# Adjacency of a graph kernel: remainders in neighbouring bf16 elements, two of sixteen one-hots on ScalarE

## What is computed

```python
# N_NODES = 3125
S = jax.ops.segment_sum(X[src], dst, num_segments=N_NODES)
Z = (1.0 + eps[l]) * X + S
```

## Time and profile before

| | us |
|---|---|
| median of three runs | 2696.34 |
| the profiled execution, its own time | 2691.28 |
| its span, first to last instruction | 2689.6 |
| building `adj`: first VectorE instruction of the loop to last ScalarE copy | 104.96 to 361.24 |

### The profile page before, as it was taken

The page is one execution under the profiler, slowest core; times in us unless marked ns, Lnnn a source line. Parts: engine busy times, 40 slices in busy tenths (PEclk is TensorE's granted clock), DMA queues, the critical chain, the costliest instruction groups (busy, mean ns, idle before and its releaser), DMA issues. The chain is left out here.

```text
span 2689.6 us, 46751 instructions
## 1 busy us (share of the span) xinstructions
PE 2128.6 (79%) x9373; PEld 1425.9 (53%) x9374; DVE 1692.9 (63%) x5215; ACT 792.3 (29%) x1810; POOL 1359.2 (51%) x1336
## 2 busy tenths in 40 slices
PE   3577768888799999998799889969996566666666
PEld 1233345555788888885455345534553444455444
DVE  7999951112677777773438634853575677777775
ACT  1233311112122222222111311132113366666663
POOL 2200000000577777771678277727782477777771
PEclk9999978888655555557899899989997777777777
DMA  0000010000444444441211011101113222222221
GB/s 10 3 0 0 0 39 0 0 0 3 120 118 119 119 118 118 119 117 52 39 17 17 9 16 17 17 9 17 17 17 111 62 65 64 66 65 64 65 65 36
DMA packets 197087, 128.42 MB, mean 48 GB/s; under 512 B 138144, under 2 KB 179993, under 8 KB 195872
## 3 DMA queue, kind: packets, MB, share of 16 engines
q0 software_dynamic: 40256, 60.21, 10.4%
q1 hardware_dynamic: 151820, 59.71, 9.0%
q10 hardware_dynamic: 4822, 6.56, 0.7%
HBM read 106.83 MB, written 13.34 MB: 45 GB/s over the span
## 5 line engine op out<-in xcount | busy, mean ns | idle before, releaser
L1742 PE MATMUL ps<-adj,extra 125*128 (+2 forms) x3150 | 607.4, 354 | 32.5 <-DVE extra L1548 32.5
L1439 POOL DMA_INDIRECT edge_rows<-pay,small x425 | 511.4, 1203 | 129.2 <-issue 127.4
L1742 PEld LDWEIGHTS ps<-adj,extra 125*128 125x128 bf16 x3150 | 309.0, 98 | 330.3 <-issue 40.3
L1921 POOL DMA_INDIRECT adj<-h_rows,adj x416 | 395.2, 950 | 135.5 <-issue 80.1
L1116 POOL DMA_INDIRECT work<-p_rows,small x416 | 395.3, 950 | 127.2 <-issue 109.2
L2098 PE MATMUL ps<-adj 128*128 128x125 f32 x928 | 206.2, 359 | 166.2 <-DVE work L1999 162.4
L1283 PE MATMUL ps<-work 128*128 x1024 | 302.7, 451 | 20.9 <-DVE work L1174 19.6
L2098 PEld LDWEIGHTS ps<-adj 128*128 128x128 f32 x928 | 169.5, 252 | 259.4 <-issue 159.6
L1294 PE MATMUL ps<-small,work 128*128 128x64 f32 x1024 | 253.1, 403 | 33.4 <-issue 32.6
L1294 PEld LDWEIGHTS ps<-small,work 128*128 128x128 f32 x1024 | 243.2, 327 | 50.0 <-issue 48.5
L1283 PEld LDWEIGHTS ps<-work 128*128 128x128 f32 x1024 | 240.3, 324 | 32.0 <-issue 29.7
(11 more groups left out here) (341 smaller groups left out, 2949.3 us busy)
## 6 DMA issues: line engine op xcount, KB each, us to landing
work<-dst_all SPq DMA_DIRECT2D x256, 64.0 KB
work<-edge_attr SPq DMA_DIRECT2D x256, 64.0 KB
edge_rows<-pay,small POOLq DMA_INDIRECT x425, 2.7
work<-p_rows,small POOLq DMA_INDIRECT x416
adj<-h_rows,adj POOLq DMA_INDIRECT x416
adj<-adj SPq DMA_DIRECT2D x232, 24.0 KB
pay<-edge_pay SPq DMA_DIRECT2D x106, 46.9 KB
work<-x_kept SPq DMA_DIRECT2D x2, 1562.5 KB, 6.6
```

Of the source, the lines that this page charges most:

```text
L1439: eng.indirect_dma_start(edge_rows[:, :], bass.IndirectOffsetOnAxis(ap=place[:, k:k + 1], axis=0), pay[:, k * ROW:(k + 1) * ROW], None).th ...
L1742: ins = eng.matmul(ps[:, j, 0:cw], parts[k][:, i * D:(i + 1) * D], cols, start=first and i == 0, stop=last and i == 2, skip_group_check=True)
L1921: eng.indirect_dma_start(gathered[:, at:at + D], None, h_rows[:, :], bass.IndirectOffsetOnAxis(ap=row3_i[:, c, DST_C:DST_C + 1], axis=0)). ...
```

## The change

Three edits, all in `adjacency`:

1. **Remainders turned.** `lows` of all four windows lie in one bf16 array with the order (window, column, chunk): the four chunks of one column are neighbours. The iota is now bf16 and written out in full (125 columns, each number four times), the remainders are copied once into bf16 with the four chunks of a window as neighbours (`low_wv`). One tensor_tensor now makes `lows` for two windows, 1000 elements, and waits until TensorE has used the second of the two. TensorE reads the stationary operand of chunk v with a step of 4 elements (8 bytes), where it read neighbours.
2. **Two of sixteen one-hots on ScalarE.** The fourth chunk (v = 3) of windows k = 0 and k = 2 of each group is made by `near`: Abs(code - key) into `far` in f16, then, behind a wait and a nop, Relu(1 - far) into `ring[k][3]`. ScalarE does this for the next group, between its wait for window k and its copy of that window. VectorE skips these two. TensorE waits for `s_near` there, and its counts of `s_code` go by 14 in a group.
3. **Constants.** GpSimd writes two more before the loop (`code16`, 500 in f16, and `one`), and `low_iota` has 500 elements and not 125. VectorE makes the negated keys (157 elements) and the turned remainders (628) before the loop.

```diff
@@ -416,14 +416,28 @@
         "key_v", "low_v", "key_c", "low_c", "over_n", "over", "place_i"))
     w_ = Words(work, 0, KEPT)
     ring = [[w_(P, WCOLS, BF16) for _ in range(F)] for _ in range(WG)]
-    lows = [w_(P, F * P, BF16) for _ in range(WG)]
-    code, base_w, low_iota = w_(P, WCOLS, I16), w_(P, NW), w_(P, P)
-    low3 = low_v.rearrange("p (v w) -> p v w", w=NW)
+    lows_all = w_(P, WG * P * F, BF16)
+    lows4 = lows_all.rearrange("p (k c v) -> p k c v", c=P, v=F)
+    lows = [lows4[:, k, :, :].rearrange("p c v -> p v c") for k in range(WG)]
+    code, base_w, low_iota = w_(P, WCOLS, I16), w_(P, NW), w_(P, P * F, BF16)
+    low_wv = w_(P, NW * F, BF16)
+    low3 = low_wv.rearrange("p (w v) -> p w v", v=F)
+    iota3 = low_iota.rearrange("p (c v) -> p c v", v=F)
     low_x, code_x = w_(P, P, BF16), w_(P, WCOLS, BF16)
+    code16, far, one, key_neg = w_(P, WCOLS, F16), [w_(P, WCOLS, F16) for _ in range(2)], w_(P, 1), w_(P, NW)
+    BY_ACT = [0, 2]
+    GA, GD = len(BY_ACT), WG * F - len(BY_ACT)
+    s_neg, s_far, s_near = sem("negated_keys_ready"), sem("distances_ready"), sem("hots_by_scalar")
+
+    def by_act(k, v):
+        return v == F - 1 and k in BY_ACT
+
+    def hots_before(k, v):
+        return sum(1 for j in range(WG) for u in range(F) if (j, u) < (k, v) and not by_act(j, u))
 
     s_const, s_code, s_used, s_kept = sem("constants_ready"), sem("hots_ready"), sem("hots_used"), sem("window_kept")
     s_over, s_x, s_sum, s_added = sem("list_loaded"), sem("listed_hot"), sem("listed_summed"), sem("listed_added")
-    s_place = sem("places_saved")
+    s_place, s_low = sem("places_saved"), sem("remainders_turned")
     GV = WG * F
 
     def groups(eng, body):
@@ -448,21 +462,30 @@
             imprecise = dict(allow_small_or_imprecise_dtypes=True)
             eng.iota(code, pattern=[[1, WCOLS]], base=0, channel_multiplier=0, **imprecise).then_inc(s_const, 1)
             eng.iota(base_w, pattern=[[WBASE, NW]], base=0, channel_multiplier=0, **imprecise).then_inc(s_const, 1)
+            eng.iota(code16, pattern=[[1, WCOLS]], base=0, channel_multiplier=0, **imprecise).then_inc(s_neg, 1)
+            eng.memset(one, 1.0).then_inc(s_neg, 1)
             eng.memset(adj_all[:, NT * N:NT * N + WN - 5], 0.0).then_inc(s_const, 1)
-            eng.iota(low_iota, pattern=[[1, P]], base=0, channel_multiplier=0, **imprecise).then_inc(s_const, 1)
+            eng.iota(low_iota, pattern=[[1, P], [0, F]], base=0, channel_multiplier=0, **imprecise).then_inc(s_const, 1)
 
         @block.vector
         def _(eng):
+            eng.tensor_scalar(key_neg, key_v[:, (F - 1) * NW:F * NW], -1.0, None, ALU.mult).then_inc(s_neg, 1)
+            eng.tensor_copy(low3, low_v.rearrange("p (v w) -> p w v", w=NW)).then_inc(s_low, 1)
+            eng.wait_ge(s_low, 1)
             eng.wait_ge(s_const, 4)
 
             def body(g, parity, n):
                 for k in range(n):
-                    eng.wait_ge(s_used, g * GV + k * F + F)
-                    at = low3[:, :, bass.ds(g * WG + k, 1)]
-                    eng.tensor_tensor(lows[k].rearrange("p (v c) -> p v c", c=P),
-                                      low_iota.unsqueeze(1).to_broadcast([P, F, P]), at.to_broadcast([P, F, P]),
-                                      ALU.is_equal)
+                    if k % 2 == 0:
+                        both = min(2, n - k)
+                        eng.wait_ge(s_used, g * GV + (k + both - 1) * F + F)
+                        at = low3[:, bass.ds(g * WG + k, both), :]
+                        eng.tensor_tensor(lows4[:, k:k + both, :, :],
+                                          iota3.unsqueeze(1).to_broadcast([P, both, P, F]),
+                                          at.unsqueeze(2).to_broadcast([P, both, P, F]), ALU.is_equal)
                     for v in range(F):
+                        if by_act(k, v):
+                            continue
 
                         at = bass.ds(g * WG + (k + v * NW), 1)
                         eng.tensor_scalar(ring[k][v], code, key_v[:, at], None, ALU.is_equal).then_inc(s_code, 1)
@@ -493,10 +516,24 @@
             for _ in range(2 * WG):
                 eng.nop(nofuse=True).then_inc(s_kept, 1)
 
+            def near(g, k):
+
+                i = BY_ACT.index(k)
+                eng.activation(far[i], code16, ACT.Abs, bias=key_neg[:, bass.ds(g * WG + k, 1)]).then_inc(s_far, 1)
+                eng.wait_ge(s_far, g * GA + i + 1)
+                eng.nop(nofuse=True)
+                eng.activation(ring[k][F - 1], far[i], ACT.Relu, scale=-1.0, bias=one).then_inc(s_near, 1)
+
+            eng.wait_ge(s_neg, 3)
+            for k in BY_ACT:
+                near(0, k)
+
             def body(g, parity, n):
                 for k in range(n):
 
                     eng.wait_ge(s_used, g * GV + k * F + F + GV)
+                    if k in BY_ACT and (not isinstance(g, int) or (g + 1) * WG + k < NW):
+                        near(g + 1, k)
                     w = g * WG + k
                     cols = min(WN, N - w * WN) if isinstance(w, int) else WN
                     out = adj[:, :, w * WN:w * WN + cols] if isinstance(w, int) else adj[:, :, bass.ds(w * WN, cols)]
@@ -515,8 +552,12 @@
 
                     eng.wait_ge(s_kept, g * WG + k + 1)
                     for v in range(F):
-                        eng.wait_ge(s_code, g * GV + k * F + v + 1)
-                        eng.matmul(ps[0:P, parity * WG + k, 0:WCOLS], lows[k][:, v * P:(v + 1) * P], ring[k][v],
+                        if by_act(k, v):
+                            eng.wait_ge(s_near, g * GA + (BY_ACT.index(k) + 1))
+                            eng.wait_ge(s_code, g * GD + hots_before(k, v))
+                        else:
+                            eng.wait_ge(s_code, g * GD + (hots_before(k, v) + 1))
+                        eng.matmul(ps[0:P, parity * WG + k, 0:WCOLS], lows[k][:, v, :], ring[k][v],
                                    start=v == 0, stop=v == F - 1).then_inc(s_used, 1)
 
             groups(eng, body)
```

## The result

The changed kernel takes 2629.11 us (median of four runs, 2627.02 to 2630.82) beside 2695.48 us of the kernel before on the same chips (four runs, 2690.97 to 2696.64). The ratio is 0.9756, with a 95% interval of 0.974 to 0.9773: 66.4 us less. 62.0 were forecast, 2634.3 us. The profiled execution's own time is 2630.21 us, its span 2628.5.

What follows compares the result with a forecast made beforehand. VectorE bounds the adj phase; afterwards ScalarE would, by a little, at 4.91 us per group. 157 windows x 0.3985 us gain 62.6, less 0.6 at the start: 2696.3 - 62.0 = 2634.3 us, range 2622 to 2662.

Steps and rivals of the forecast that it cites:

- The bound: Phase building adj, before the change: VectorE, busy for all 240.00 us, sets the pace at 1.626 us per window.
- VectorE's 4.81 us: VectorE's load per group of four windows: fourteen one-hots, 3.63 us, plus two comparisons of 0.59 (4.29 to 5.87).
- The one open term, 0.59 between 0.33 and 1.12: VectorE's comparison of 1000 two-byte elements: 0.59 us at two elements per step, 1.12 at one.
- ScalarE's 4.91 us: ScalarE's load per group, two Abs and Relu pairs plus four copies: just above VectorE's, so ScalarE becomes the bound.
- The gap between Abs and Relu: ScalarE's wait and nop between the two instructions: 0.13 us, with 0.03 and 0.23 as ends.
- two copies: ScalarE's copies in the loop: 0.51 us each, four per group.
- The start: Constants made before the loop: VectorE's loop begins at about 105.55 and not 104.96, costing 0.6 us (0 to 1.5).
- TensorE at nothing: Sixteen matmuls per group, about 3.5 us, stay below 4.9 us; weight loads stay near 133 ns, so no cost.
- rival C: TensorE's weight loads at 8-byte steps grow and are no longer hidden: up to 8.66 us per group, 2781 us; chance 0.04.
- A: VectorE's comparison stays at one element per step: 5.87 us per group, 2672 us; chance 0.12.
- B: ScalarE does not overlap its instructions: 5.50 us per group, 2657 us; chance 0.17, including anything between it and the forecast.
- the 0.67 us forecast for L483: Sign in the changed profile: VectorE's comparison of 1000 elements shows a mean duration of 0.67 us, or 1.20 at one element per step.

Runs made afterwards that it cites:

- the third experiment: Changed kernel with two-byte remainders but chunks not turned, so each remainder is read 125 times with step 0: 2666.72 us, ratio 0.99.
- the last experiment: Changed kernel with GpSimd writing the turned iota first and two constants needed only later last: 2628.17 us, ratio 0.975.

## Why the prediction was right

**The bound**, VectorE's queue before the change, held. In the experiments that change a load, the group follows the sum of VectorE's terms, or ScalarE's where that is larger, to 0.03 us, with terms read from the changed kernel: 5.32, 5.98, 5.84, 5.05, 6.13 and 4.94 measured, 5.32, 5.97, 5.84, 5.07, 6.16 and 4.93 worked out.

**VectorE's 4.81 us** was 4.80. The one open term, 0.59 between 0.33 and 1.12, was 0.59, and the third experiment shows both what it needs and that the upper end was real. The Trainium skill (VectorE: DVE Perf Modes, "The perf-mode tier table") gives a `tensor_tensor` two rates, the double one for bf16 in SBUF. The runs show both, 0.26 us per 500 elements when turned and 0.52 when not (0.59 and 1.11 per 1000, less the 0.07 of the instruction), but by the table alone the third experiment, all bf16, would have had the double rate, and its comparison took 1205 ns: the type alone doesn't decide.

**ScalarE's 4.91 us** was the step that failed: it is 4.74, and so VectorE stays the bound and not ScalarE. The prediction had named this outcome, a loop of 4.8 us with the gap or the copies priced too high, and it was both. Two terms were too large. The gap between Abs and Relu is 0.09 us and not 0.13, since a nop costs ScalarE 0.05 and not the 0.10 that I had taken from VectorE's rows (0.08 per group with its two pairs); and two copies take 0.95 and not 1.02 (0.14 per group). Abs and Relu themselves were 0.01 or so too short. Of the 0.17 us per group only the 0.11 down to VectorE's load counts: 39.25 x 0.11 = 4.3 us more gained. That the two loads are near each other, and that ScalarE's latency is of no account, was right; because they are so near, the wrong engine as the bound hardly moved the forecast time.

**The start** cost 1.55 us and not 0.6, for two reasons. The turned iota takes 1.17 us where I took 0.56. And I let the comparison start as soon as the iota had ended (105.5 and 105.55), though the rows of before have 0.37 us between the two; it is 0.45 here. So the corrected sum is 62.0 + 4.3 - 0.95 = 65.4 us; the phase shows 64.8, and the medians 66.4. The 1.6 us between these two can't be told from scatter: the part behind the phase, the same in all kernels, varies by more (2319.2 to 2330.8).

**TensorE at nothing** was right in the sum and wrong in its row: loads near 133 ns were forecast and they take 192, so the rule that the prediction cites under C, by which a step of 8 bytes leaves the load as it is, was not borne out. 0.19 us is also the length from which, if nothing hid it, rival C would have made the kernel slower than it was. The loads are hidden, even at 317 ns. I had also expected VectorE to be idle for a few us and TensorE to wait for Relu; in the changed kernel's loop neither happened.

**The rivals.** A is what the third experiment built, at its price (239.41 us of phase, 39.9 more than the changed kernel). B (ScalarE without overlap) did not come: a copy lasts 589 ns and the next instruction starts 0.475 us after it. Giving a one-hot to GpSimd, which is idle here, was not tried. C did not come at 8, 16 or 24 bytes. The rule of the Trainium skill that relu and add belong on VectorE (ScalarE: Activation LUTs, "Rules for kernel authors") compares engines one by one: per one-hot VectorE is 5.5 times faster (0.26 against 1.42 us for the pair), and yet each one-hot given away gained 0.26 us per group, until the third, which lost 1.34.

## What to carry to other kernels

When one engine bounds a loop, write down the load of every engine per round, start to start, and move work until two of them are level; the next piece moved after that costs nearly its full price on the other engine (1.34 of 1.42 us here). When a comparison of two-byte elements reads one operand again and again, try real neighbours innermost and the repetition outside: here the same elements then went at twice the rate, and the strided read that this leaves to TensorE's weight load was hidden behind matmuls of 500 columns. An engine without idle time need not be the bound: look whether its round is shorter than its neighbour's, so that it only works off a backlog, and shorten it to see whether anything follows.

## What the runs showed of the hardware

- Weight loads of 125 bf16 columns last 133 ns at a step of 2 bytes, 192 at 8, 317 at 16 and 302 at 24, and even at the two longest steps the phase did not grow by more than 0.5 us (200.04 and 199.77 beside 199.55).
- TensorE began the changed phase at the pace of its lower level, 1.2 GHz, though the profile gives the granted clock as 1.00. Weight loads, and busy times of the stretch around them:

```profile
108.16 0.23 PEld L560 LDWEIGHTS ps<-work 125*125 125x125 bf16 x1 [0.19 <-issue]
108.58 0.23 PEld L560 LDWEIGHTS ps<-work 125*125 125x125 bf16 x1 [0.19 <-DVE work L491]
108.99 0.23 PEld L560 LDWEIGHTS ps<-work 125*125 125x125 bf16 x1 [0.19 <-DVE work L491]
...
111.91 4.34 PEld L560 LDWEIGHTS ps<-work 125*125 125x125 bf16 x20 [0.19 <-issue]
```

```profile
107.00:117.00 10.00, 9.51 (x33) 6.62 (x33) 10.00 (x35) 7.28 (x13) 0.00 (x0) 1.00 0.01 2
```

  Loads 0.415 us apart, one per matmul of 500 columns, are that level; twenty of them in 4.34 us, from 111.91 on, are about 0.22 apart, the upper one. Before its first matmul TensorE had been idle for 11 us. ScalarE waited for TensorE until 112.55 (0.68 us) and then not again until 294.55, so its backlog dates from the windows that TensorE caught up on. The kernel before starts in the same way, with loads 0.42 us apart up to 111.00. A phase that starts at the upper level was not tried.
- GpSimd's iota of 500 elements took 0.55 us in one run of columns and 1.17 (1.19 in the last experiment) with each number four times. VectorE's copy beside it does not explain this: it overlaps the iota for 0.31 us in the changed kernel and for 1.09 in the last experiment. Nor does the type by itself: 125 numbers take 0.24 us in f32 and in bf16 (third experiment). That leaves the repetition within the pattern, which was not tried alone.
- The durations recorded for L491 grew, within the phase and from kernel to kernel, 343 to 471 ns in the changed kernel (means of 352 with no one-hot on ScalarE, 374 without the nop and 420 in the changed kernel), while the distance from start to start stayed at 0.26 us. So the cost is read from the distance, not from such a duration; the 0.67 us forecast for L483 was recorded as 0.747 although its distance is the 0.59 us of the sum.
